# Routing by one scan with ScalarE making half of the token tables, and the weights of layers 2 and 3 set up inside neighbouring stages

## The chip, the cores and the metric

The kernel runs on one core of a Trainium2 chip. The metric is the device time of one execution in microseconds (us), lower is better. The kernel before takes 7486.76 us, the median of three runs from 7485.75 to 7492.47.

The engines are TensorE (PE, with its weight loads as PEld), VectorE (DVE), ScalarE (ACT), GpSimd (POOL) and SyncE (SP, which here only issues DMAs).

## The reference, cut to what matters

A graph network of four layers on 3125 nodes with 256 features and 50,000 edges. Each layer adds a graph convolution and a linear-attention mixer to `x`, and then a mixture of experts. Only the parts below are touched.

```python
# every layer ends in experts; layer 1 keeps 1 expert per token, the others 2
def moe(x, gate_w, gate_b, w1, b1, w2, b2):          # 8 experts, 16 in layer 2
    logits = x @ gate_w + gate_b
    vals, idx = top_k(weights_of(logits), TOP)
    # layer 1 only: pos = cumsum(one_hot) - 1; kept = pos < capacity
    return sum(vals[:, k] * expert[idx[:, k]](x) for k in range(TOP))

# layer 2 (graph part): h = x @ Wn.T + bn; the score of an edge needs sum(h[src] * attn)
# layer 3 (graph part), for l in range(2), 32 heads of 8, two edge types:
#   k = x @ Wk[l]; q = x @ Wq[l]; v = x @ Wv[l]
#   kw = k[src] times Watt[l] of the edge's type;  m = v[src] times Wmsg[l] of that type
#   a  = (kw * q[dst]).sum(-1) * pri[l, type] / sqrt(8); softmax over the edges of dst
#   h  = (softmax-weighted sum of m) @ Wa[l]
#   x  = h * sigmoid(skip[l]) + x * (1 - sigmoid(skip[l]))
```

The kernel folds the attention vector of layer 2 into a column of the node weights (`w[:, :, D+1] = sum(Wn * attn)`), and the small matrices of layer 3 into its node weights (`Wk` times the block-diagonal `Watt`, `Wv` times the block-diagonal `Wmsg`), so that one matmul over the nodes makes the whole table that the edges gather from. These folds are the "set-up" in this document.

## The kernel before

The program is a sequence of phases (`Phase`). A phase opens on-chip memory and semaphores and mostly holds one block, in which each engine has its own instruction list; at the end of a block all engines meet. Once more than 90 semaphores have been used up, the next phase begins with two more meetings, between which POOL clears them (L89 to L91). There is no planner: the order on each engine is the order in which the code issues, and engines wait for each other by semaphores only.

The 3125 nodes lie as 25 tiles of 125 partitions (`NT`, `P`). The order of stages is: layer 0 (edge sort, two graph passes), experts 0, layer 1, experts 1, layer 2, experts 2, layer 3 (two graph passes and a mixer), experts 3. The experts are `moe` (L2138), in this order:

- `settle` (a call of `renew`, L1804; names f0_in, f1_in, f2_in, f3_in, of which the profile shows f_in): per tile the mixer's matmul, the layer norm, the gate's logits. SP first loads the gate's weights, and then per tile stores the normalised rows to DRAM (L1888, L1889). DVE, ACT and PE take turns on each tile.
- `choose` (L2195) on DVE alone: maximum and index per tile, one-hot tables `oh`, their sum `ohs`, and the running count of tokens per expert over the tiles, `before`, by 25 additions with a drain after each (L2224 to L2227).
- `rank`: three matmuls and a run of small DVE instructions, which give each token its place in the list ordered by experts.
- `invert` (L2306): turns places into the list of tokens. DVE makes `hot` (which column of the list, one long comparison, L2330) and then, in five parts, `low` (which row, L2335) and `high` (L2339), that is `hot` times the tile's number and `hot` times the row's number within the tile, one instruction per half and per k. After each part PE runs its matmuls over `low` and `high` (L2322). DVE then copies the sum out and combines the halves (L2344, L2346).
- `experts`: POOL gathers the tokens (L2389), SP loads the weights, PE, ACT and DVE work through the tiles of 128 tokens.
- `fetch` (`renew` again): POOL gathers each node's results, and the next layer's table is made.

The set-up of layer 2 (`open_layer2`, L2881) stands between the end of layer 1 and f1_in, as phases of their own: two small fills (L2888), three loads by SP (`move`, L1119), a fourth load, and the fold on DVE (`attended`, L1360 to L1372). The set-up of layer 3 (`open_layer3`, L3019) stands between the end of layer 2 and f2_in: POOL makes two masks (`head_mask`, L1654), SP issues 30 loads and waits for them (L1129), POOL makes `hot` (L3049), ACT the sigmoid (L3052), PE and DVE `pcol` (L1688, L1701), and in the phase `l3_prod` DVE makes 16 products of mask and matrix (L3066) and scales 8 of them (L3072), PE runs 32 matmuls in eight groups (L3089), and DVE and ACT copy the groups out by turns (L3079, L3096).

## Time and profile before

| | |
|---|---|
| median of three runs | 7486.76 us |
| the profiled execution | 7480.89 us |
| its span | 7479.1 us |
| busy share of PE, PEld, DVE, ACT, POOL | 68, 48, 64, 38, 47% |
| mean granted TensorE clock | 0.856 of full speed |

The stretches that the change touches, as the timeline gives them, in us from the start of the span:

| stretch | from | to | length |
|---|---|---|---|
| experts 0: f0_in; choose and rank; invert | 2285.6 | 2388.7 | 103.1 |
| layer 2 set-up | 3288.0 | 3300.4 | 12.4 |
| experts 1: f1_in; choose and rank; invert | 3300.4 | 3370.0 | about 70 |
| layer 3 set-up | 4435.4 | 4479.5 | 44.1 |
| experts 2: f2_in; choose and rank; invert | 4479.5 | 4580.4 | 100.9 |
| experts 3: choose and rank; invert | 7184.4 | 7233.2 | 48.8 |

The profile is one execution, with every instruction's start and duration. Busy shares are averages over a sequence of stages with different limits, so for a change like this one it is the timeline of each stretch that matters: who works, who waits, and what the next phase waits for.

### The profile page before, as it was taken

To read this page: it belongs to the slowest core of one execution; us is meant where nothing else is said; L and a number is where in the kernel's file an instruction comes from. 1 tells how busy PE (TensorE), PEld (TensorE's weight loads), DVE (VectorE), ACT (ScalarE), POOL (GpSimd) and SP (SyncE) were. 2 spreads that over 40 slices of the span, in tenths; PEclk is the share of its full clock that TensorE was granted. 3 is DMA by queue.
4 is the path that set the end of the run, shared out by engine and by line. 5 is a ranking of instruction groups with operands and counts; after the bars stand their busy time and mean duration, and the time that the engine had idled before them with its cause. 6 is when DMAs were issued, how large, how long until landed. Compare 5 with 4: busy or idle time off the path is not lost. (4 is left out here: it accounts for less than half of the span.)

```text
span 7479.1 us, 108245 instructions
## 1 busy us (share of the span) xinstructions
PE 5106.3 (68%) x21553; PEld 3606.0 (48%) x21554; DVE 4782.9 (64%) x12016; ACT 2809.2 (38%) x6885; POOL 3492.6 (47%) x3516
## 2 busy tenths in 40 slices
PE   4763677767774967759666656967776867776764
PEld 4762444444444834548543345834444444444453
DVE  6875477677776168551556554169997459996453
ACT  2551355345524220012223212227775147772321
POOL 1775277447730267731167701136664046661014
PEclk9999877777777988979867778989998999997777
DMA  3442244334422943338334405947765157772036
GB/s 88 163 144 62 78 129 127 81 89 128 127 58 88 318 113 101 104 72 323 117 96 108 104 16 175 301 144 213 211 210 157 36 161 212 211 212 57 20 110 202
DMA packets 523816, 1021.67 MB, mean 137 GB/s; under 512 B 143645, under 2 KB 284498, under 8 KB 514846
## 3 DMA queue, kind: packets, MB, share of 16 engines
q0 software_dynamic: 191360, 489.21, 24.3%
q1 hardware_dynamic: 301663, 497.07, 20.8%
q10 hardware_dynamic: 30528, 32.52, 1.2%
q8 instruction: 87, 1.43, 0.1%
q14 instruction: 178, 1.46, 0.1%
HBM read 927.97 MB, written 90.27 MB: 136 GB/s over the span
## 5 line engine op out<-in xcount | busy, mean ns | idle before, releaser
L733 POOL DMA_INDIRECT l_hgt_ep_g<-l_tkm,l_hgt_ep_ix x832 | 922.6, 1109 | 440.7 <-PE l_hgt_ep_out L831 235.4
L744 POOL DMA_INDIRECT l_gat_ep_g<-l_gat_th,keep_e_src x832 | 861.6, 1036 | 433.8 <-issue 229.7
L831 PE MATMUL l_gat_ep_out<-l_gat_ep_g,l_gat_ep_here 128*126 128x264 f32 x1664 | 711.7, 572 | 140.1 <-DVE l_gat_acc L988 136.0
L831 PEld LDWEIGHTS l_gat_ep_out<-l_gat_ep_g,l_gat_ep_here 128*126 128x126 f32 x1664 | 393.0, 267 | 367.5 <-DVE l_gat_acc L988 299.0
L2438 DVE TENSOR_TENSOR f_moe_experts_yb<-f_moe_experts_py,f_moe_experts_b2s 128x256 f32<-128x256 f32 x208 | 88.3, 424 | 709.9 <-PE f_moe_experts_py L2421 687.6
L2389 POOL DMA_INDIRECT f_moe_experts_xg<-f_moe_tx,f_moe_tok x208 | 196.7, 945 | 734.6 <-PE f_moe_experts_px L2402 618.0
L831 PE MATMUL l_hgt_ep_out<-l_hgt_ep_g,l_hgt_ep_here 128*126 128x288 f32 x1664 | 499.5, 424 | 53.2 <-DVE l_hgt_ep_g L974 52.0
L2453 ACT ACTIVATE f_moe_experts_ht<-f_moe_experts_phid,f_moe_experts_b1b 128x128 f32<-128x128 f32 x848 | 241.3, 372 | 726.8 <-PE f_moe_experts_phid L2412 720.1
L872 ACT COPY l_gat_ep_stage<-l_gat_ep_out 30x264 f32<-30x264 f32 x832 | 307.5, 371 | 537.6 <-PE l_gat_ep_out L831 529.1
L525 POOL DMA_INDIRECT recs<-place_stage,place_pos x392 | 425.2, 1085 | 138.5 <-issue 117.7
L2710 POOL DMA_INDIRECT l_edges_g<-l_table,keep_e_src x416 | 409.7, 985 | 147.5 <-issue 120.3
L2412 PE MATMUL f_moe_experts_phid<-f_moe_experts_xt,f_moe_experts_w1b 128*128 128x128 f32 x3392 | 430.7, 281 | 66.9 <-DMA f_moe_experts_b1b<-in_L_ffn_b 63.3
L744 POOL DMA_INDIRECT l_ep_g<-l_table,keep_e_src x416 | 403.7, 970 | 126.6 <-issue 122.0
L2412 PEld LDWEIGHTS f_moe_experts_phid<-f_moe_experts_xt,f_moe_experts_w1b 128*128 128x128 f32 x3392 | 403.5, 195 | 90.6 <-issue 60.3
L805 PE MATMUL l_hgt_ep_found<-l_q,l_hgt_ep_hot 125*128 x1664 | 427.2, 401 | 23.8 <-ACT l_hgt_ep_hot L848 18.7
L831 PE MATMUL l_ep_out<-l_ep_g,l_ep_here 128*126 128x257 f32 x832 | 333.1, 553 | 106.8 <-DVE l_acc L988 99.6
L2421 PE MATMUL f_moe_experts_py<-f_moe_experts_w2b,f_moe_experts_ht 128*128 128x256 f32 x1696 | 400.0, 380 | 0.0
L872 ACT COPY l_hgt_ep_stage<-l_hgt_ep_out 126x288 f32<-126x288 f32 x832 | 307.4, 394 | 218.0 <-PE l_hgt_ep_out L831 207.3
L988 DVE TENSOR_TENSOR l_gat_acc<-l_gat_acc,l_gat_ep_out 125x264 f32 x832 | 343.9, 413 | 68.6 <-issue 48.8
L988 DVE TENSOR_TENSOR l_hgt_acc<-l_hgt_acc,l_hgt_ep_stage 125x288 f32 x832 | 369.6, 444 | 24.3 <-ACT l_hgt_ep_stage L872 17.4
L831 PEld LDWEIGHTS l_hgt_ep_out<-l_hgt_ep_g,l_hgt_ep_here 128*126 128x126 f32 x1664 | 284.6, 190 | 180.1 <-issue 132.5
L2722 PE MATMUL l_edges_out<-l_edges_g,l_edges_here 128*125 128x256 f32 x832 | 258.1, 461 | 147.9 <-DMA l_edges_g<-l_table,keep_e_src 46.3
(635 smaller groups left out, 11735.3 us busy)
## 6 DMA issues: line engine op xcount, KB each, us to landing
l_hgt_ep_hot<-locrow SPq DMA_DIRECT2D x208, 256.0 KB, 5.0
f_moe_experts_w1b<-in_L_ffn_w SPq DMA_DIRECT2D x32, 1024.0 KB
f_moe_experts_w2b<-in_L_ffn_w SPq DMA_DIRECT2D x32, 1024.0 KB
f_moe_experts_w1b<-in_L_ffn_w SPq DMA_DIRECT2D x64, 512.0 KB
f_moe_experts_w2b<-in_L_ffn_w SPq DMA_DIRECT2D x64, 512.0 KB
f_moe_experts_w1b<-in_L_ffn_W SPq DMA_DIRECT2D x56, 512.0 KB, 4.9
f_moe_experts_w2b<-in_L_ffn_W SPq DMA_DIRECT2D x56, 512.0 KB, 5.1
l_gat_ep_hot<-locrow SPq DMA_DIRECT2D x104, 256.0 KB
```

Source lines behind the costliest of these rows:

```text
L525: gp.indirect_dma_start(recs, bass.IndirectOffsetOnAxis(ap=pos[:, b, j:j + 1].bitcast(U32), axis=0), stage[:, b, j, :], None).then_inc(sca ...
L733: gp.indirect_dma_start(g[:, b % NB, j, 0:W], None, table, bass.IndirectOffsetOnAxis(ap=ix[:, b, j:j + 1].bitcast(U32), axis=0)).then_inc( ...
L744: gp.indirect_dma_start(g[:, k % NB, j, 0:W], None, table, bass.IndirectOffsetOnAxis(ap=idx[:, k * CT + j:k * CT + j + 1].bitcast(U32), ax ...
L805: mm = pe.matmul(found[:, h, j * D:j * D + D], hot[0:P, b % 2, 128 * (h * HT + j):128 * (h * HT + j) + 128], look[:, bass.ds(blks[h * HT + ...
L831: pe.matmul(out[:, t % 4, 0:WO], here[:, b % 2, t, :], g[:, b, t, F:F + WO], start=True, stop=True).then_inc(s_out, 1)
L872: act.copy(stage[lo:P + 1, b % 2, t, :], out[lo:P + 1, t % 4, 0:WO]).then_inc(s_staged, 1)
L988: v.tensor_tensor(slot, slot, stage[0:P, b % 2, t, :] if kind == "hgt" else out[0:P, t % 4, 0:WO], ALU.add).then_inc(s_added, 1)
L2412: mm = pe.matmul(phid[:, b % 2, 128 * f:128 * f + 128], w1b[:, b, k, 128 * f:128 * f + 128], xt[:, b % 2, k, :], start=(k == 0), stop=(k = ...
L2421: mm = pe.matmul(py[:, b % 2, 0:D], ht[:, b % 2, f, :], w2b[:, b, f, :], start=(f == 0), stop=(f == FC - 1))
L2453: act.activation(ht[:, b % 2, f, :], phid[:, b % 2, 128 * f:128 * f + 128], func, bias=b1b[:, b, f:f + 1])
L2710: gp.indirect_dma_start(g[:, i % RB, j, :], None, table, bass.IndirectOffsetOnAxis(ap=core.e_src[:, i * EG + j:i * EG + j + 1].bitcast(U32 ...
L2722: pe.matmul(out[:, j, 0:D], here[:, i % 4, j, :], g[:, i % RB, j, :], start=True, stop=True).then_inc(s_out, 1)
```

## The change

1. Running counts: `before` is laid out expert by expert with one leading zero each, and made by one `tensor_tensor_scan` (state times `going` plus `coming`; `going` is 0 at each expert's first column and 1 elsewhere). The two matmuls that read `before` now read it with a stride.
2. Token tables: ACT makes the half of `high` that holds the row number, one instruction per part, as soon as `hot` stands (`s_high`); DVE keeps the other half. PE waits for both.
3. Layer 2: the four loads are issued by SP at the head of f1_in, behind the gate's; the fills and the fold stand at the end of f1_in's DVE list.
4. Layer 3: the 30 loads are issued by SP at the head of f2_in, behind the gate's; everything else stands inside the invert phase of experts 2. POOL makes masks and the 16 products, ACT the sigmoid, `pcol`, all scalings and all eight copies, PE the matmul for `pcol` ahead of its token matmuls and the 32 others behind them.

```diff
 def renew(..., square=None, beside=None):
@@ SP's list, after the gate's loads
+                if beside is not None:
+                    beside["load"](sp)
...
@@ end of DVE's list
+            if beside is not None and "last" in beside:
+                beside["last"](v)
+                v.drain()
...
@@ choose
+                v.memset(coming[:, :, 0:1], 0.0)
+                v.memset(going[:, :, :], 1.0)
+                come = coming[:, :, 1:NT + 1].rearrange("p e t -> p t e")
                 if TOP == 2:
                     v.tensor_tensor(ohs[:, :, :], oh[:, 0, :, :], oh[:, 1, :, :], ALU.add)
+                    v.tensor_tensor(come, oh[:, 0, :, :], oh[:, 1, :, :], ALU.add)
                 else:
                     v.tensor_copy(ohs[:, :, :], oh[:, 0, :, :])
-                v.memset(before[:, 0, :], 0.0)
-                v.drain()
-                for t in range(NT):
-                    v.tensor_tensor(before[:, t + 1, :], before[:, t, :], ohs[:, t, :], ALU.add)
-                    v.drain()
+                    v.tensor_copy(come, oh[:, 0, :, :])
+                v.drain()
+                v.memset(going[:, :, 0:1], 0.0)
+                v.drain()
+                v.tensor_tensor_scan(before[...], going[...], coming[...], 0.0, ALU.mult, ALU.add)
+                v.drain()
...
@@ rank
-                    pe.matmul(pa[:, 0:NT * NE], core.ones[0:P, 0:P], before[:, 0:NT, :].rearrange("p t e -> p (t e)"), ...)
-                    pe.matmul(pb[:, 0:NE], core.ones[0:P, 0:P], before[:, NT, :], start=True, stop=True).then_inc(s_mm, 1)
+                    pe.matmul(pa[...], core.ones[0:P, 0:P], before[:, :, 0:NT].rearrange("p e t -> p t e"), ...)
+                    pe.matmul(pb[:, 0:NE], core.ones[0:P, 0:P], before[:, :, NT], start=True, stop=True).then_inc(s_mm, 1)
...
@@ invert
+                @block.scalar
+                def _(act):
+                    if making is not None:
+                        making["act_first"](act, p_col)
+                    act.wait_ge(s_high, 1)
+                    for q in range(NQ):
+                        act.activation(high[:, q, :, 1, :], hot[:, q * TQ * TOP:(q + 1) * TQ * TOP, :], ACT.Copy, scale=core.iotap[0:P, 0:1]).then_inc(s_rowed, 1)
+                    if making is not None:
+                        making["act_last"](act, p_prod)
                 @block.tensor
                 def _(pe):
+                    if making is not None:
+                        making["tensor_first"](pe, p_col)
                     for q in range(NQ):
                         pe.wait_ge(s_hot, q + 1)
+                        pe.wait_ge(s_rowed, q + 1)
...
+                    if making is not None:
+                        making["tensor"](pe, p_prod)
                 @block.vector
-                    v.tensor_scalar(ids[:, :, 1], core.ones[0:P, 0:NT], core.iotap[0:P, :], None, ALU.mult)
...
-                        for w in range(2):
-                            for k in range(TOP):
-                                v.tensor_tensor(high[:, q, k::TOP, w, :], hot[...], ids[..., w:w + 1]..., ALU.mult)
+                        for k in range(TOP):
+                            v.tensor_tensor(high[:, q, k::TOP, 0, :], hot[...], ids[...]..., ALU.mult)
...
@@ open_layer2: the phases l2_one, l2_w_in and l2_att give way to load (4 DMAs) and
+    def fold(v):
+        count_column(v)
+        v.wait_ge(s_in, 64)
+        v.tensor_tensor(tmp[:, :, :], w[:, :, 0:D], arow[:, :].unsqueeze(1).to_broadcast([128, 2, D]), ALU.mult)
+        v.drain()
+        v.tensor_reduce(w[:, :, D + 1:D + 2], tmp[:, :, :], AX.X, ALU.add)
+        v.drain()
+        v.tensor_tensor(tmp[0:P, 0, :], b[:, 0:D], arow[0:P, :], ALU.mult)
+        v.drain()
+        v.tensor_reduce(b[:, D + 1:D + 2], tmp[0:P, 0, :], AX.X, ALU.add)
...
@@ open_layer3: the phases l3_m8a, l3_m8b, l3_in, l3_hot, l3_alpha, l3_pcol and l3_prod give way to
+    def load(sp):
+        for to, src in pairs:                      # the same 30 transfers
+            sp.dma_start(to, src).then_inc(s_in, 16)
+    def on_pool(gp):
+        gp.affine_select(out=hot..., in_=core.ones[0:16, :]..., ...).then_inc(s_hot, 1)
+        # two memsets and four affine_selects for the masks, then
+        gp.wait_ge(s_mask, 2)
+        gp.wait_ge(s_in, 16 * len(pairs))
+        for l in range(2):
+            for i in range(2):
+                for t in range(2):
+                    for c in range(2):
+                        gp.tensor_tensor(bd[:, l, i, t, c, :]..., m8[:, i, :]..., tt[:, l, i, t, c, :]..., ALU.mult).then_inc(s_bd, 1)
+    def on_tensor_first(pe, p_col):
+        pe.wait_ge(s_hot, 1)
+        pe.wait_ge(s_in, 16 * len(pairs))
+        pe.matmul(p_col[:, 0:8], hot[:, :], pri[...], start=True, stop=True).then_inc(s_pcol, 1)
+    def on_tensor(pe, p_prod):
+        for n in range(8):
+            l, r, t = n // 4, n // 2 % 2, n % 2
+            if n % 4 == 0:
+                pe.wait_ge(s_scaled, 4 * (l + 1))
+                pe.wait_ge(s_bd, 8 * (l + 1))
+            if n >= 4:
+                pe.wait_ge(s_out, n - 3)
+            ...                                    # the same 4 matmuls as before, into p_prod[:, n % 4]
+            mm.then_inc(s_mm, 1)
+    def on_act_first(act, p_col):
+        act.wait_ge(s_in, 16 * len(pairs))
+        act.activation(alpha[:, :, 0], alpha[:, :, 0], ACT.Sigmoid)
+        act.wait_ge(s_pcol, 1)
+        act.copy(pcol[:, :], p_col[:, 0:8])
+        act.drain()
+        act.activation(alpha[:, :, 1], alpha[:, :, 0], ACT.Identity, bias=core.ones[:, 0:1], scale=-1.0)
+    def on_act_last(act, p_prod):
+        for l in range(2):
+            act.activation(wa[l][:, :, :], wa[l][:, :, :], ACT.Copy, scale=alpha[:, l, 0:1])
+            act.wait_ge(s_bd, 8 * l + 4)
+            # four products of l scaled by their column of pcol, each .then_inc(s_scaled, 1)
+        for n in range(8):
+            act.wait_ge(s_mm, n + 1)
+            act.copy(w[n // 4][...], p_prod[:, n % 4, :]).then_inc(s_out, 1)
+        act.drain()
```

## Rows read from the trace of the kernel before

**Rows 1.** Windows: busy us of PE, PEld, DVE, ACT, POOL; clock, DMA share, GB/s.

```profile
4435.40:4479.50 44.10, 10.01 (x66) 9.75 (x66) 8.88 (x33) 3.83 (x6) 2.41 (x7) 0.57 0.18 50
...
4479.50:4528.00 48.50, 45.97 (x300) 38.90 (x300) 33.72 (x151) 37.85 (x101) 0.00 (x0) 1.00 0.24 68
...
2285.00:2341.00 56.00, 50.67 (x300) 40.28 (x300) 41.79 (x176) 38.34 (x101) 0.31 (x1) 0.96 0.21 59
...
4558.00:4581.00 23.00, 6.24 (x50) 4.92 (x50) 19.72 (x30) 0.00 (x0) 0.00 (x0) 0.50 0.00 1
```

**Rows 2.** The timeline of layer 3's set-up: start, duration, engine, line, operation.

```profile
4428.60 6.83 DVE L3005 SCALAR_TENSOR_TENSOR keep_x<-l_acc,keep_x 125x6400 f32<-125x6400 f32 x1
...
4436.03 0.40 POOL L1667 TENSOR_SCALAR_AFFINE_SELECT l_m8a_b<-l_m8a_a 128x128 f32<-128x128 f32 x1
...
4438.62 0.83 SPq L1129 DMA_DIRECT2D l_alpha<-in_L_gnn_skip  x2
...
4451.97 0.98 SPq L1129 DMA_DIRECT2D l_wa<-in_L_gnn_Wa  x2
...
4469.14 9.44 PE L3089 MATMUL l_prod_acc<-l_mats_bd,l_mats_wt 128*128 128x128 f32 x64 [7.34 <-DVEq L3073]
...
4478.62 0.59 ACT L3096 COPY l_w<-l_prod_acc 128x512 f32<-128x512 f32 x1 [1.20 <-PE l_prod_acc L3089]
...
4479.51 0.37 SPq L1871 DMA_DIRECT2D f_moe_gate_gw<-in_L_ffn_gate_w  x1
```

**Rows 3.** The timeline of layer 2's set-up.

```profile
3281.14 6.83 DVE L2871 SCALAR_TENSOR_TENSOR keep_x<-l_acc,keep_x 125x6400 f32<-125x6400 f32 x1
...
3297.55 0.69 DVE L1363 TENSOR_TENSOR l_tmp<-l_w,l_arow 128x512 f32<-128x512 f32 x1 [9.09 <-PEq L95]
...
3300.36 0.37 SPq L1871 DMA_DIRECT2D f_moe_gate_gw<-in_L_ffn_gate_w  x1
```

**Rows 4.** The timeline of the running counts, experts 0 and 2.

```profile
2353.03 5.97 DVE L2226 TENSOR_TENSOR f_moe_route_before<-f_moe_route_before,f_moe_route_ohs 125x8 f32<-125x8 f32 x25
...
4536.47 6.17 DVE L2226 TENSOR_TENSOR f_moe_route_before<-f_moe_route_before,f_moe_route_ohs 125x16 f32<-125x16 f32 x25
```

**Rows 5.** The groups of DVE, by shape: the scans of two lengths.

```profile
L1070 DVE TENSOR_TENSOR_SCAN l_gat_ej_fwd<-l_gat_ej_rule,l_gat_ej_vals 4x832 f32<-4x832 f32 x2 | 3.8, 1878 | 0.2
...
L936 DVE TENSOR_TENSOR_SCAN l_gat_ep_top<-l_gat_ep_masks,l_gat_ep_fwd 32x128 f32<-32x128 f32 x104 | 43.0, 413 | 9.7 <-issue 0.4
```

**Rows 6.** The timeline of the invert phases of experts 0, 1 and 2.

```profile
2372.82 1.52 DVE L2339 TENSOR_TENSOR f_moe_invert_high<-f_moe_invert_hot,f_moe_invert_ids 125x280 bf16<-125x280 bf16 x4
...
3362.46 0.55 DVE L2339 TENSOR_TENSOR f_moe_invert_high<-f_moe_invert_hot,f_moe_invert_ids 125x160 bf16<-125x160 bf16 x2
...
4558.42 0.23 DVE L2329 TENSOR_SCALAR f_moe_invert_ids<-keep_ones,keep_iotap 125x25 f32<-125x25 f32 x1
...
4563.53 1.69 DVE L2339 TENSOR_TENSOR f_moe_invert_high<-f_moe_invert_hot,f_moe_invert_ids 125x320 bf16<-125x320 bf16 x4
...
4578.17 1.25 PE L2322 MATMUL f_moe_invert_tok<-f_moe_invert_high,f_moe_invert_low 125*128 125x128 bf16 x10 [1.97 <-DVEq L2341]
...
4580.39 0.35 ACTq L2445 DMA_DIRECT2D f_moe_experts_b2s<-in_L_ffn_b  x1
```

**Rows 7.** The groups of ACT, by shape.

```profile
L846 ACT ACTIVATE l_gat_ep_hot<-l_gat_ep_hot,keep_minusp 128x1024 bf16<-128x1024 bf16 x104 | 119.3, 1148 | 51.6 <-DMA l_gat_ep_hot<-locrow 49.2
```

**Rows 8.** The timeline of layer 3's first graph pass, POOL beside DVE.

```profile
5104.42 1.22 DVE L974 TENSOR_TENSOR l_hgt_ep_g<-l_hgt_ep_g 128x1024 f32<-128x1024 f32 x1
...
5104.71 1.74 POOL L733 DMA_INDIRECT l_hgt_ep_g<-l_tkm,l_hgt_ep_ix  x1 [0.30 <-issue]
...
5106.76 0.95 POOL L733 DMA_INDIRECT l_hgt_ep_g<-l_tkm,l_hgt_ep_ix  x1 [0.30 <-issue]
```

**Rows 9.** The timeline: PE's first mixer matmuls in f0_in and in f2_in.

```profile
2286.85 2.07 PE L1933 MATMUL f_in_out<-keep_mix_a,f_in_xt 128*125 128x256 f32 x4
...
4480.48 1.13 PE L1933 MATMUL f_in_out<-keep_mix_a,f_in_xt 128*125 128x256 f32 x4 [0.30 <-ACT f_in_xt L1974]
```

More of the change, by code:

```diff
@@ L3043, in open_layer3 @@
              + [(wa[l][:, :, :], ins["L3_gnn_Wa"][l].rearrange("(k p) m -> p k m", p=128)) for l in range(2)])
-        with Phase(core, "l3_hot") as p2:
-            block = p2.block()
-            @block.gpsimd
-            def _(gp):
-                gp.affine_select(out=hot[:, :].rearrange("h (b w) -> h b w", w=8), in_=core.ones[0:16, :].rearrange("h (b w) -> h b w", w=8),
-                                 compare_op=ALU.is_equal, fill=0.0, base=0, pattern=[[-1, 16], [0, 8]], channel_multiplier=1)
-                gp.drain()
@@ new lines, in on_tensor_first @@
+    def on_tensor_first(pe, p_col):
+        pe.wait_ge(s_hot, 1)
+        pe.wait_ge(s_in, 16 * len(pairs))
+        pe.matmul(p_col[:, 0:8], hot[:, :], pri[:, :, :].rearrange("h l c -> h (l c)"), start=True, stop=True).then_inc(s_pcol, 1)
+    def on_tensor(pe, p_prod):
[6 more added lines that the diff above has]
+                pe.wait_ge(s_out, n - 3)
+            for i in range(2):
+                for c in range(2):
+                    mm = pe.matmul(p_prod[:, n % 4, D * i + 128 * c:D * i + 128 * c + 128], wt[:, l, i, c, 128 * r:128 * r + 128], bd[:, l, i, t, c, :],
+                                   start=True, stop=True)
+            mm.then_inc(s_mm, 1)
@@ new lines, in on_act_first @@
+    def on_act_first(act, p_col):
[9 more added lines that the diff above has]
+            act.wait_ge(s_bd, 8 * l + 4)
+            for t in range(2):
+                for c in range(2):
+                    at = 4 * l + 2 * c + t
+                    act.activation(bd[:, l, 0, t, c, :], bd[:, l, 0, t, c, :], ACT.Copy, scale=pcol[:, at:at + 1]).then_inc(s_scaled, 1)
+        for n in range(8):
+            act.wait_ge(s_mm, n + 1)
+            act.copy(w[n // 4][:, n // 2 % 2, 512 * (n % 2):512 * (n % 2) + 512], p_prod[:, n % 4, :]).then_inc(s_out, 1)
+        act.drain()
@@ L3186, in build @@
             o = open_layer2(core, p2) if last > 4 else None
-            layer1_ffn(core, settle("f1_in", {}), fetch("f1_out", 4, o))
+            layer1_ffn(core, settle("f1_in", {"beside": o["fold"]} if o else {}), fetch("f1_out", 4, o))
             if last == 4:
@@ L3193, in build @@
         with Phase(core, "l3") as p3:
-            o = open_layer3(core, p3) if last > 6 else None
-            layer2_ffn(core, settle("f2_in", source), fetch("f2_out", 6, o))
+            with Phase(core, "l3_brief") as p3b:
+                o = open_layer3(core, p3, p3b) if last > 6 else None
+                making = o["making"] if o else None
+                layer2_ffn(core, settle("f2_in", {**source, "beside": making} if making else source), fetch("f2_out", 6, o), making)
             if last == 6:
```

142 lines of the change are left out of this document (65 added, 77 removed).

## The prediction

> **What bounds the kernel now.** Everything the change touches stands in serial stretches, where one engine works and the others wait at the end of the phase, so shares over the span say nothing. I read the windows first, then the timeline of each stretch, and then looked up prices for new instructions in the groups by shape. In the windows the reader is to see three kinds of stretch [rows 1]. The layer 3 set-up, 44.1 us, has no engine busy above 10.0 us: it is a chain of hand-overs and a wait for DMAs. Invert 2, 23.0 us, is DVE alone: 19.7 us of DVE, 6.2 of PE, nothing on ACT and POOL, at the half level of the clock (0.50, 1.2 GHz). f2_in, 48.5 us, is PE-heavy (46.0 us) at the full level. The edge passes, most of the span, are not touched.
>
> **Layer 3 set-up: what goes.** It runs from the end of the last DVE pass, 4428.60 + 6.83 = 4435.43, to f2_in's first instruction at 4479.51 [rows 2]: 44.1 us. One meeting of the engines stays (4478.62 + 0.59 to 4479.51, 0.3 us). Gone: 43.8 us. Three costs come back.
>
> SP in f2_in: 30 issues now stand ahead of the stores of the normalised rows. They took 4438.62 to 4452.95, 0.48 us each [rows 2], 14.3 us. Nobody in f2_in waits for a store, only the gathers behind invert 2 do. With 50 stores at the same price SP needs 80 x 0.48 = 38 us in a stage of 48.5 us, and ends in time. Cost 0; if the issues were slower by more than a quarter, SP would end last and each further tenth would cost 4 us.
>
> The cover of PE's clock: f2_in today follows the set-up's 9.4 us of matmuls and starts at the full level, afterwards PE comes from at least 7 us of idleness beside DVE's last pass (it has no work there). f0_in starts like that: its first four mixer matmuls take 2.07 us against 1.13 in f2_in [rows 9], and its stage has 0.96 of the clock on average [rows 1]. Cost 1.0 us, with 0 and 3 as ends.
>
> The matmuls of the products: they now start when the last token matmul of invert 2 is done, and end the phase. Today the run from their first start to the next phase, 4469.14 to 4479.51, takes 10.4 us, the change of the clock level within it included [rows 2]. It takes the place of the tail from 4578.17 + 1.25 to 4580.39, 1.0 us [rows 6], in which DVE's two last instructions stood; these fall in its shadow. Cost 9.4 us; 8.5 if the token matmuls before have already brought the clock up, 18 if it stays at the half level.
>
> **Layer 2 set-up.** From 3281.14 + 6.83 = 3287.97 to 3300.36, 12.4 us, less one meeting of 0.3 [rows 3]: 12.1 us go. The fold, 3297.55 to 3300.36 less the meeting, 2.5 us, and two fills of 0.1 in all come back at the end of f1_in's DVE list, where DVE is last anyway: fully on the path. Its loads were issued 30 us before, and four more issues at 0.48 on SP's queue fit ahead of the first store. Gain 9.5 us, 8.5 to 9.9.
>
> **Running counts.** 25 additions with their drains: 5.97 us with 8 experts, 6.17 with 16 [rows 4]; a fill of 0.1 goes with them. New are a second sum, written expert by expert, two more fills, a drain, and the scan. The trace has scans: 832 columns in 1.88 us, 128 in 0.413 [rows 5], so 2.08 ns a column, and 0.58 us for 8 x 26 = 208, 1.01 us for 416. The sum: 0.24 us for the smallest instruction with its drain (5.97/25) and 1.07 ns a column (6.83/6400) [rows 2] give 0.45 for 200 and 0.67 for 400. The rest is 0.4 with the scan's drain. With 8 experts 6.07 - 1.43 = 4.6 us, with 16 6.27 - 2.08 = 4.2 us: 3 x 4.6 + 4.2 = 18.0 us. All of it is on the path: PE waits in the next phase. Two unknowns: the sum's strided write and the strided read of `before` by PE. No row has either; if each took twice its time, 0.5 us per expert stage would be lost, so 16 to 18.5.
>
> **Token tables.** DVE's `high` takes 1.52 us per part in experts 0 (and 3, the same shape), 0.55 in experts 1, 1.69 in experts 2 [rows 6]. Half goes, five times, and the second column of `ids` with it (0.1): 3.9 + 3.9 + 1.5 + 4.3 = 13.6 us. ACT must keep up: 1024 columns in bf16 take it 1.148 us [rows 7], so 640 at most that, and by columns 0.72 us; DVE still needs 1.4 for `low` and 0.8 for its half, 2.2 per part, and ACT starts as soon as `hot` stands. ACT finishes each part first even at 1.15 us. Ends: 0 gain if ACT took over 3 us, 14.
>
> **Invert 2, four engines at once.** ACT's first piece (sigmoid with its table load, the `pcol` copy) needs about 2.5 us, and `hot` alone holds ACT back for 3.6 us, so it hides. POOL: two fills and five masks at 0.40 [rows 2], 2.4 us, then 16 products. The trace has no product on POOL. From below a mask of the same size, 0.40 us; from above 1.74 us, a POOL instruction that a DVE instruction stretched [rows 8]. I take 0.5, nearest to the mask, so POOL would end at 10.4 us of the phase. PE needs the first half of the products (and ACT's four scalings, at most 0.4 each) when the token matmuls end: 4578.17 + 1.25 - 4558.4 = 21.0 us today, less 4.3, so at 16.7, and the second half five us later. Products of up to 1.2 us would hide.
>
> But they do not run alone. A POOL instruction started 0.3 us after a DVE product of two on-chip tensors takes 1.74 us where its like takes 0.95, also beside other DVE work: it ends 0.95 - 0.14 us after that DVE instruction did [rows 8]. DVE's `hot`, `low` and `high` are of that kind, 16 instructions, and POOL reads on-chip too in 20 of its own. The row shows POOL held, not DVE. If only POOL is held and gets in between DVE's instructions, it ends late, at about 19 to 22 us, and PE waits 0 to 2 us. If DVE is held as well, once per instruction, 16 x 0.45 = 7 us go onto its path. I take 4 us, the ends are 0 and 8.
>
> The Trainium skill has a rule for this, and it speaks against the change: SBUF — State Buffer, section "Who interferes with whom", says that a VectorE instruction with two SBUF inputs contends with a GpSimd instruction that reads SBUF, and that whichever starts first has the shared pair to itself until it ends. The trace agrees for one direction, with 1.74 against 0.95 us; by the rule DVE is held too, which is the end of 7 us above. GPSIMD Engine Reference, section 3.1, gives a two-input product on GpSimd as 1.96 times VectorE's time; no run here shows it so far, and by it the products would still be under 1.2 us, with the sum unchanged.
>
> Clearing of semaphores: the change uses some ten more semaphores and has fewer phases, so a clearing moves and perhaps one is added; none to two of about 2 us, both signs; I take 0.
>
> **The sum.** Layer 3: 43.8 - 9.4 - 1.0 - 4.0 = 29.4. Layer 2: 9.5. Counts: 18.0. Tables: 13.6. Together 70.5 us. The profiled execution took 7480.9 us (its span is 7479.1), so it would take 7410.4. It lay 5.9 us below the median of 7486.8; against that median the forecast is 7416.3, and I say 7416. Under 0.2% (15 us) a measurement of this kernel can hardly tell from no change; the forecast is five times that.
>
> **The rivals.**
> A, the sum, with POOL and DVE holding each other up by 0 to 8 us: 7410 to 7423. Chance 0.68.
> B, ACT becomes the bound of the token tables, or the split buys nothing, because ACT reads and writes these strided rows at over 2 us a part. Against it stand 1.148 us for 1024 columns [rows 7]. 13.6 us less: 7430. Chance 0.06.
> C, PE stays at the half level in f2_in. For it: the idleness before. Against it: f0_in, with the same work per tile after a longer wait, had 0.96 on average [rows 1]. At the half level its 46 us of PE work take up to 2.07/1.13 times as long [rows 9], 84 us instead of 46, 38 us more: 7454. Chance 0.04.
> D, the level of the long graph passes moves by itself, in either direction, for a reason that this trace can't tell beforehand: I allow 15 us either way. It speaks against this that none of their instructions is touched. Chance 0.19.
> E, slower: POOL's chain ends invert 2. Its end is 2.4 + 16 T + 5.6 us after the phase's start (T a product, 5.6 half of the 9.44 us of matmuls with the last copy and the meeting), against 31 us in my sum (22.0 - 1.0 - 4.3 + 10.4 + 4). It costs from T = 1.4 on and has eaten the whole gain at T = (31 + 70.5 - 8)/16 = 5.8 us, over three times the longest price above, even with each product behind a `low` of 1.4 us. With T = 7 the kernel would take 7505. Chance 0.03.
>
> The range: A from 7408 and D's half on either side, B inside, C and E left out: 7399 to 7438. Faster by over 0.2%: A, B, C, most of D, 0.95. Within 0.2%: 0.03. Slower: 0.02 to 0.03, with E.
>
> **What would show it.** The groups: the 100 additions of the running counts gone and four scans in their place, of 0.6 and 1.0 us. The timeline: f1_in starts 0.3 to 0.4 us after layer 1's last DVE pass and f2_in after layer 2's; f1_in has a tail of 2.6 us on DVE. In invert 0 and 3 DVE's parts come every 2.3 us instead of 3.05, and PE waits for DVE, not for ACT. In invert 2 the start of the products' matmuls, 16.7 us after the phase's start if nobody holds DVE, up to 24 if it is held; POOL's products 0.4 to 0.6 us when alone, and 1 to 2 us where they start inside a `low`. The windows: clock near 1.00 in f2_in. I would be wrong if ACT or POOL, not DVE, released PE's first matmul in an invert phase, if f2_in grew by more than 3 us, or if an edge pass changed by more than 5.

## The result, and the profile after

The changed kernel takes 7430.15 us (median of 4 runs, 7422.14 to 7436.22), the kernel before, timed with it, 7487.92 us (4 runs, 7485.75 to 7492.47): a ratio of 0.9918, 95% interval 0.9906 to 0.9931. So 57.8 us are gained where 70.5 were forecast; 7430 lies inside the forecast's range of 7399 to 7438, 14 us above its 7416 and outside the 7410 to 7423 of its main case, rival A. By the interval the gain is 52 to 70 us. The profiled execution of the changed kernel took 7426.5 us, its span 7424.3, the mean granted clock 0.857 against 0.856.

The windows of the changed stages (start and end; length; busy us and count of PE, PEld, DVE, ACT, POOL; granted clock, DMA share, GB/s): invert 0, f1_in with its fold, f2_in, invert 2, invert 3.

```profile
2367.60:2386.20 18.60, 5.58 (x50) 4.39 (x50) 14.70 (x19) 3.37 (x5) 0.00 (x0) 0.50 0.00 0
3282.50:3323.50 41.00, 29.37 (x150) 28.86 (x150) 26.76 (x137) 29.34 (x78) 0.00 (x0) 0.50 0.34 99
4416.80:4467.30 50.50, 48.12 (x300) 40.87 (x300) 33.78 (x152) 38.01 (x101) 0.00 (x0) 0.94 0.38 108
4494.20:4523.00 28.80, 15.11 (x116) 13.76 (x116) 18.23 (x19) 13.94 (x27) 20.08 (x23) 0.62 0.00 1
7154.60:7171.50 16.90, 5.58 (x50) 4.39 (x50) 14.71 (x19) 3.37 (x5) 0.00 (x0) 0.50 0.00 1
```

Invert 2 now has all four engines at work; it took 22.1 us, from 4558.3 to 4580.4 (its window in [rows 1] is drawn a little wider), and takes 28.8. f2_in went from 48.8 to 50.5 us and from a clock of 1.00 to 0.94 [rows 1].

The timeline where the two set-ups stood (start, duration, engine, line, operation; in brackets the idle time before it and what ended it): the end of layer 1 and f1_in, then the end of layer 2 and f2_in.

```profile
3275.37 6.83 DVE L2905 SCALAR_TENSOR_TENSOR keep_x<-l_acc,keep_x 125x6400 f32<-125x6400 f32 x1
3282.53 0.39 SPq L1871 DMA_DIRECT2D f_moe_gate_gw<-in_L_ffn_gate_w  x1
...
3315.97 0.69 DVE L2937 TENSOR_TENSOR l_tmp<-l_w,l_arow 128x512 f32<-128x512 f32 x1
...
3317.99 0.42 DVE L2943 TENSOR_REDUCE l_b<-l_tmp 125x1 f32<-125x256 f32 x1
...
4409.67 6.83 DVE L3055 SCALAR_TENSOR_TENSOR keep_x<-l_acc,keep_x 125x6400 f32<-125x6400 f32 x1
4416.81 0.40 SPq L1871 DMA_DIRECT2D f_moe_gate_gw<-in_L_ffn_gate_w  x1
...
4418.03 2.07 PE L1935 MATMUL f_in_out<-keep_mix_a,f_in_xt 128*125 128x256 f32 x4
```

From the end of the DVE pass to the next stage there are now 0.3 us in both places, against 44.1 [rows 2] and 12.4 [rows 3]. The last line also shows the cold start of f2_in: 2.07 us for its first four matmuls, as f0_in had it [rows 9].

The running counts, experts 0 (208 columns) and experts 2 (416), where [rows 4] had 5.97 and 6.17 us: the second sum and the scan.

```profile
2357.35 0.54 DVE L2231 TENSOR_TENSOR f_moe_route_coming<-f_moe_route_oh 125x200 f32<-125x200 f32 x1
...
2358.14 0.59 DVE L2238 TENSOR_TENSOR_SCAN f_moe_route_before<-f_moe_route_going,f_moe_route_coming 125x208 f32<-125x208 f32 x1
...
4475.68 0.89 DVE L2231 TENSOR_TENSOR f_moe_route_coming<-f_moe_route_oh 125x400 f32<-125x400 f32 x1
...
4476.83 1.02 DVE L2238 TENSOR_TENSOR_SCAN f_moe_route_before<-f_moe_route_going,f_moe_route_coming 125x416 f32<-125x416 f32 x1
```

The timeline of invert 2. The reader is to see three things: the two masks of POOL (L3107) that end only after DVE's `hot` (the first 0.26 us after it, the second as long after the first `low`), the pairs of `high` at 1.41 us, and the products' matmuls (L3137) that start behind the last token matmul and end the phase.

```profile
4494.42 3.48 DVE L2365 TENSOR_TENSOR f_moe_invert_hot<-keep_iota,f_moe_route_hi 125x3200 bf16<-125x3200 f32 x1
...
4494.82 4.92 POOL L3107 TENSOR_SCALAR_AFFINE_SELECT l_brief_wide<-l_brief_wide 128x128 f32<-128x128 f32 x2
...
4497.93 3.70 ACT L2344 ACTIVATE f_moe_invert_high<-f_moe_invert_hot,keep_iotap 125x640 bf16<-125x640 bf16 x5 [1.88 <-DVE f_moe_invert_hot L2365]
...
4500.88 13.49 POOL L3119 TENSOR_TENSOR l_brief_bd<-l_brief_m,l_brief_tt 128x128 f32<-128x128 f32 x16
...
4502.06 1.41 DVE L2373 TENSOR_TENSOR f_moe_invert_high<-f_moe_invert_hot,f_moe_invert_ids 125x320 bf16<-125x320 bf16 x2
...
4512.49 1.25 PE L2356 MATMUL f_moe_invert_tok<-f_moe_invert_high,f_moe_invert_low 125*128 125x128 bf16 x10 [1.73 <-DVEq L2375]
4512.75 1.28 ACT L3156 ACTIVATE l_brief_bd<-l_brief_bd,l_brief_pcol 128x128 f32<-128x128 f32 x4 [5.39 <-POOL l_brief_bd L3119]
4513.53 8.48 PE L3137 MATMUL f_moe_invert_p_prod<-l_brief_bd,l_brief_wt 128*128 128x128 f32 x64
...
4522.06 0.58 ACT L3159 COPY l_w<-f_moe_invert_p_prod 128x512 f32<-128x512 f32 x1 [0.31 <-PE f_moe_invert_p_prod L3137]
4522.97 0.35 ACTq L2479 DMA_DIRECT2D f_moe_experts_b2s<-in_L_ffn_b  x1
```

In all invert phases it is DVE (the queue entry behind `high`, L2375) that releases PE; in invert 2 ACT's five instructions take 3.70 us together, 0.74 each, and are done with the last part while DVE makes its second.

**Stage by stage.** I cut both timelines at the first instruction of each stage. The stretches that the change touches, in us (before minus after): running counts with the rank phases behind them 4.8, 4.0, 3.2, 4.8 = 16.8; inverts 0, 1 and 3, 2.1, -0.3 and 3.7; set-ups 12.1 and 42.8; the ends paid for them -2.1 (f1_in), -1.7 (f2_in) and -6.7 (invert 2). That is 66.7. The clearing of semaphores (L90), six times in both kernels, has moved from the experts to the ends of inverts 0 and 1 (1.6 us each, so these lose 3.7 and 1.3 in truth), and from the layer 3 set-up to the end of layer 2's pass, 1.7 us. With these put right the change removes 68 us by the stretches it touches, where the span fell by 54.8. The untouched stretches grew by 13 in sum. Layer 3's two graph passes, called hgt0 and hgt1 below, moved against each other, in the kernel before and in the changed one:

```profile
5033.70:5777.00 743.30, 513.83 (x1872) 320.49 (x1872) 663.38 (x1145) 515.03 (x1249) 486.63 (x518) 0.97 0.68 203
6060.50:6790.40 729.90, 508.55 (x1872) 316.82 (x1873) 663.30 (x1145) 513.21 (x1248) 486.43 (x518) 0.99 0.70 206
...
4974.40:5711.50 737.10, 513.90 (x1872) 320.52 (x1872) 662.90 (x1145) 514.60 (x1249) 493.58 (x518) 0.97 0.69 204
5996.60:6735.40 738.80, 513.06 (x1872) 320.79 (x1872) 663.85 (x1145) 514.18 (x1248) 485.88 (x518) 0.98 0.69 204
```

hgt0 is 6.2 us shorter, 1.7 of it a clearing that has moved out of it into the stage before; hgt1 is 8.9 longer. Of the others experts 3 grew most, by 6.3 us, at 267 GB/s against 277, and experts 2 shrank by 3.7. Where this comes from is what the experiments ask, besides the contention in invert 2.

### The profile page after: what moved, and what is told of

Its sections match the earlier page's. It is cut to its first block and busy times, and to the rows that moved or that the text cites. A ratio compares the mean times of both kernels' runs of the same rounds, so it can differ in the third digit from the quotient of the medians.

```text
span 7424.3 us, 107945 instructions
## 1 busy us (share of the span) xinstructions
PE 5125.7 (69%) x21553; PEld 3617.6 (49%) x21554; DVE 4752.9 (64%) x11861; ACT 2828.9 (38%) x6921; POOL 3525.0 (47%) x3532
## 5 line engine op out<-in xcount | busy, mean ns | idle before, releaser
L805 PE MATMUL l_hgt_ep_found<-l_q,l_hgt_ep_hot 125*128 x1664 | 431.2, 404 | 25.5 <-ACT l_hgt_ep_hot L848 20.6
L805 PEld LDWEIGHTS l_hgt_ep_found<-l_q,l_hgt_ep_hot 125*128 125x128 f32 x1664 | 310.5, 197 | 99.2 <-issue 62.0
```

The source lines that it names most:

```text
L805: mm = pe.matmul(found[:, h, j * D:j * D + D], hot[0:P, b % 2, 128 * (h * HT + j):128 * (h * HT + j) + 128], look[:, bass.ds(blks[h * HT + ...
```

## The experiments

Each is timed against the kernel before on the same chip in the same series; "stretch" is the time between the first instructions of two stages in the one profiled execution.

**Four parts alone**, each on the kernel before: the choose and rank edits; the invert edits without the layer 3 work; the loads and fold of layer 2; those of layer 3, with DVE still making both halves of `high`:

```diff
+                        for w in range(2):
+                            for k in range(TOP):
+                                v.tensor_tensor(high[:, q, k::TOP, w, :], hot[:, q * TQ * TOP + k:(q + 1) * TQ * TOP:TOP, :],
+                                                ids[:, q * TQ:(q + 1) * TQ, w:w + 1].to_broadcast([P, TQ, TT]), ALU.mult)
```

> The kernel before with the running counts alone changed (scan in the four choose phases). Theory S (the gain is the sum of the touched stretches): the stretches choose to rank of the two profiles say 4.6 + 4.2 + 3.3 + 4.9 = 17.0 us, the forecast said 18.0; so 16 to 18 us under the kernel before, 7470 +- 3, and the passes hgt1 and experts 3 as in the kernel before, within 3 us. Rival D (the drift of the untouched passes comes with the change): hgt1 +8.9 and experts 3 +6.3 us again, and the time only 2 to 8 us under the kernel before.

> The kernel before with the token tables alone split between VectorE and ScalarE. The forecast's term is 13.6 us; the stretches of the two profiles had 2.1 (invert 0), -0.3 (invert 1) and 3.7 us (invert 3), with a clearing of semaphores of about 1.6 us that had moved into inverts 0 and 1. Theory S: the clearing is elsewhere here, so 3.7 + 1.3 + 4.0 + 3.7 = 12.7 us, time 10 to 14 us under the kernel before. Rival B (the split buys little where ScalarE is slow): under 6 us. Rival D: drift of hgt1 and experts 3 by +15 us, time the same as before.

> The kernel before with the layer 2 set-up alone moved into f1_in. Theory S: -12.1 us in front of f1_in, +2.1 to 2.6 at its end, so 9.5 to 10 us under the kernel before. Rival (f1_in's stores come late behind the four loads, or drift): 5 us or less.

> The kernel before with the layer 3 set-up alone moved (loads in f2_in, products in invert 2, VectorE still making both halves of the token tables). Theory S: -42.8 us in front of f2_in, +1.7 in f2_in; invert 2 grows by 28.8 - 22.1 + 4.0 = 10.7 us if the table split and the making add up, so 28 to 31 us under the kernel before. VectorE is held by GpSimd only while it makes one half more per part: if each two-input instruction is held once, 2 us more. Rival D (the drift belongs to the moved weights of layer 3: hgt1 +8.9, experts 3 +6.3): 15 us under the kernel before.

| part alone | stretches, clearings put right, us | by the measured time, us | ratio, 95% interval |
|---|---|---|---|
| counts | -17.7 | -14.2 | 0.9982 (0.9973 to 0.9991) |
| token tables | -12.3 | +4.2 | 1.0007 (0.9997 to 1.0017) |
| layer 2 | -10.0 | +4.6 | 1.0005 (0.9996 to 1.0014) |
| layer 3 | -26.3 | -20.6 | 0.9977 (0.9966 to 0.9988) |

Three of the four came as theory S had them (17.0, 12.7 and 9.5 to 10 us), layer 3 did not, with 26.3 us for 28 to 31: choose -4.7, -4.5, -3.4, -4.9; inverts of the tables -2.1 (a clearing of 1.6 in it), -1.0, -3.8, -3.7; the gap before f1_in gone and +2.1 behind it; the gap before f2_in -42.6, f2_in +1.4, invert 2 +12.9. They add up to -66.3, close to the 68 of the whole. The time does not: the parts give -26.0 together, against -57.8 for the whole, and the tables and layer 2 give nothing that can be measured. By the intervals the gain is 7 to 20 us for the counts, which holds their 17.7 (the median, 7469.9, is the 7470 expected), at most 2 for the tables, 3 for layer 2 and 25 for layer 3; these three lie under their stretches. Rival B is out, since ACT's split saved what was expected in its stretches. What eats the gain stands in passes without an edited instruction. The windows of layer 2's graph pass, in the kernel before and with the tables alone:

```profile
3762.30:4352.70 590.40, 377.70 (x1044) 230.31 (x1044) 355.02 (x1154) 166.71 (x471) 403.68 (x416) 0.69 0.38 96
```

```profile
3753.80:4355.90 602.10, 384.55 (x1044) 234.92 (x1044) 355.29 (x1154) 166.71 (x471) 404.05 (x416) 0.67 0.37 94
```

The same 1044 matmuls, 1154 DVE and 416 POOL instructions take 11.7 us longer (1.7 of it a clearing that now stands at the end), at a clock of 0.67 against 0.69 and with the same DVE and POOL time. The expectation for p_counts that hgt1 and experts 3 stay within 3 us failed: +6.5 and +6.5.

In p_l3 invert 2 grew by 12.9 us, not 10.7 (the 2 us more that its expectation allowed if each instruction is held), and its DVE rows give the price of the contention. First a part with POOL's products running, then the last one, when they had ended (4533.66 + 13.41 = 4547.07):

```profile
4543.24 1.54 DVE L2359 TENSOR_TENSOR f_moe_invert_low<-keep_iota,f_moe_route_lo 125x1280 bf16<-125x1280 f32 x1
4544.70 2.72 DVE L2363 TENSOR_TENSOR f_moe_invert_high<-f_moe_invert_hot,f_moe_invert_ids 125x320 bf16<-125x320 bf16 x4
4547.54 1.49 DVE L2359 TENSOR_TENSOR f_moe_invert_low<-keep_iota,f_moe_route_lo 125x1280 bf16<-125x1280 f32 x1
4548.95 1.69 DVE L2363 TENSOR_TENSOR f_moe_invert_high<-f_moe_invert_hot,f_moe_invert_ids 125x320 bf16<-125x320 bf16 x4
```

So four `high` cost 1.03 us more beside POOL, 0.26 each, and a `low` 0.05.

**The changed kernel again, and its work moved further.** after_again has no edit. pool_early starts POOL's list in f2_in; choose also takes the rest out of invert 2; choose110 is choose with fewer clearings:

```diff
+        if beside is not None and "pool" in beside:      # in renew (f2_in)
+            @block.gpsimd
+            def _(gp):
+                beside["pool"](gp)
...
-                        making["pool"](gp)                # in invert
```

```diff
+            with Phase(core, f"{name}_choose") as pc:     # choose, beside DVE's list
...
+                        making["act_first"](act, p_col)
+                        making["act_last"](act, p_prod)
...
+                        making["tensor_first"](pe, p_col)
+                        making["tensor"](pe, p_prod)
...
-        if len(self.core.spent) > 90:                     # choose110
+        if len(self.core.spent) > 110:
```

> The changed kernel once more, nothing edited. The four parts alone gave 14.2, -4.2, -4.6 and 20.6 us, 26.0 together, against 57.8 for the whole and about 65 for the touched stretches of the two profiles. Theory N (the edge and expert passes scatter from execution to execution by 10 us and more, a stretch that the change touches does not): the touched stretches repeat within 0.5 us, the untouched ones of the same kernel differ by up to 10 us each way, and the time is 50 to 65 us under the kernel before. Rival F (each kernel has its own fixed offset in the untouched passes): hgt1 +8.9 and experts 3 +6.3 us repeat within 2 us.

> The changed kernel with GpSimd's masks and its 16 products moved out of invert 2 into f2_in, where it has nothing to do. Theory H (VectorE is held in invert 2 by GpSimd's products, about 0.5 us in four to five parts): invert 2 goes from 28.8 to 26.0 to 26.6 us, the last token matmul comes 2.3 us earlier, and f2_in, bound by TensorE, grows by less than 1 us; time 1 to 3 us under the changed kernel. Rival (the longer periods come from ScalarE or TensorE, not from GpSimd): the periods of VectorE's parts stay at 2.95 us and invert 2 at 28.8. Second rival: GpSimd holds VectorE in f2_in as well, and that stage grows by over 2 us.

> As the last, and ScalarE's scalings, the 32 product matmuls and the copies of their results moved out of invert 2 into the choose phase in front of it, where TensorE and ScalarE are idle for 14.5 us. Theory: invert 2 is then the token tables alone, 22.1 - 4.3 = 17.8 to 18.5 us instead of 28.8; the choose phase must hold sigmoid and pcol (2 us), eight scalings and 9.5 us of matmuls at the half level, about 14 to 16 us against 14.5, so 0 to 2 us more. Net 9 to 11 us under the changed kernel, 7420 by its own median. Rival: the matmuls run at the half level for the whole and end at 18 us, so choose grows by 4 us and 6 to 7 are left.

> As the last, with the spent semaphores cleared when over 110, not 90, have gathered, so fewer clearings. Theory: each clearing is two meetings and a clearing, about 1.6 us, all on the path; one or two of six go and none need stand in an invert phase, 1.5 to 3.5 us less than the last. Rival: the clearings lie in places where something else is waited for (a DMA) and the time does not change.

| | median us | runs from, to | ratio to before (7483.02), 95% interval |
|---|---|---|---|
| after_again | 7429.39 | 7426.64, 7433.21 | 0.9929 (0.9916 to 0.9943) |
| pool_early | 7421.65 | 7410.30, 7429.95 | 0.9920 (0.9907 to 0.9934) |
| choose | 7415.02 | 7409.15, 7420.36 | 0.9907 (0.9892 to 0.9922) |
| choose110 | 7418.92 | 7402.91, 7431.69 | 0.9915 (0.9901 to 0.9929) |

after_again: the touched stretches repeat within 0.1 us; of the untouched ones hgt1 repeats (738.8 both times), experts 2 is 4.0 longer, experts 3 2.3 shorter, layer 2's pass 2.6 longer. Both theories had a part right. Two profiles of one kernel differ by a few us per pass, but hgt1's excess over the first profile of before (8.9) returned in after_again, choose (9.1), p_tables (9.8), p_l2 (7.8), pool_early (7.5) and p_counts (6.5), and was 2.9 in p_l3 and 0.8 in choose110. In the same runs hgt0, the clearing put right, came 3.4 to 5.4 us shorter, and 0.5 in choose110. The two passes together are 1.4 to 6.3 us longer than in the first profile of before, 0.2 in choose110, and in p_l3 2 shorter: most of hgt1's excess stands against hgt0, and hgt1 alone does not explain the missing gain.

pool_early, the timeline: POOL's products in f2_in, then the last part of invert 2 and PE's matmuls.

```profile
4438.31 6.68 POOL L3120 TENSOR_TENSOR l_brief_bd<-l_brief_m,l_brief_tt 128x128 f32<-128x128 f32 x16 [19.56 <-DMA l_wa<-in_L_gnn_Wa]
...
4509.23 0.89 DVE L2374 TENSOR_TENSOR f_moe_invert_high<-f_moe_invert_hot,f_moe_invert_ids 125x320 bf16<-125x320 bf16 x2
...
4510.20 1.25 PE L2357 MATMUL f_moe_invert_tok<-f_moe_invert_high,f_moe_invert_low 125*128 125x128 bf16 x10 [1.17 <-DVEq L2376]
4511.24 9.50 PE L3138 MATMUL f_moe_invert_p_prod<-l_brief_bd,l_brief_wt 128*128 128x128 f32 x64
```

With POOL away a pair of `high` is back at 0.89 us from 1.41, the period of a part at 2.41 from 2.98, and the last token matmuls come 15.7 us after the phase's start, not 18.35: theory H, with 2.6 us. The phase shrinks only by 1.6, for the products' matmuls now take 9.50 us against 8.48. The windows show why, first two of the changed kernel, then two of pool_early:

```profile
4513.50:4515.80 2.30, 2.30 (x14) 2.30 (x12) 0.59 (x2) 0.74 (x3) 0.86 (x3) 0.50 0.00 0
4515.90:4522.60 6.70, 6.12 (x55) 5.93 (x53) 0.00 (x0) 4.33 (x8) 0.00 (x0) 1.00 0.00 0
...
4511.20:4515.70 4.50, 4.50 (x24) 4.50 (x22) 0.52 (x2) 1.17 (x2) 0.00 (x0) 0.50 0.00 0
4515.80:4521.30 5.50, 4.93 (x45) 4.74 (x43) 0.00 (x0) 3.46 (x6) 0.00 (x0) 1.00 0.00 0
```

The granted clock rises to the full level at nearly the same time in both, 21.7 and 21.2 us after the phase's start, so the matmuls that now come earlier run at the half level. By the measured time pool_early is 7.7 us under after_again, with overlapping runs; the 1.1 us of its stretches are below what that can tell. f2_in grew by 0.5 us. POOL's products alone take 0.42 us each from start to start, 0.84 in invert 2.

choose: the windows of f2_in, the choose phase and invert 2.

```profile
4413.90:4465.50 51.60, 48.84 (x300) 41.08 (x300) 34.31 (x152) 38.22 (x102) 8.77 (x23) 0.93 0.37 106
4465.50:4483.40 17.90, 10.22 (x67) 10.00 (x67) 10.72 (x89) 11.53 (x24) 0.00 (x0) 0.77 0.00 1
4495.00:4512.90 17.90, 6.24 (x50) 4.92 (x50) 15.53 (x19) 3.70 (x5) 0.00 (x0) 0.50 0.00 0
```

Invert 2 is at 17.9 us as expected, but the choose phase grew by 3.4 us, which is nearer to the rival's 4: ACT did the sigmoid, its table load and the scaling of `wa` first, and PE started only 3.7 us into the phase. By the measured time choose is 14.4 us under the changed kernel of the same series, and their runs do not overlap; its stretches account for 8 of them. choose110 saved its 1.6 us in invert 0 and in invert 1 and one clearing in all, but by the measured time it is no faster than choose (the runs overlap): 1.7 us are below what that can tell.

**Controls on the kernel before, and the best version.** before_again has no edit; b_110 only the new threshold; b_double makes the additions twice; best is choose with ACT's order changed and the threshold at 125:

```diff
-                for t in range(NT):                      # b_double
+                for t in [*range(NT), *range(NT)]:
                     v.tensor_tensor(before[:, t + 1, :], before[:, t, :], ohs[:, t, :], ALU.add)
```

```diff
-        act.activation(alpha[:, :, 0], alpha[:, :, 0], ACT.Sigmoid)
         act.wait_ge(s_pcol, 1)
         act.copy(pcol[:, :], p_col[:, 0:8])
...
                     act.activation(bd[:, l, 0, t, c, :], bd[:, l, 0, t, c, :], ACT.Copy, scale=pcol[:, at:at + 1]).then_inc(s_scaled, 1)
+        act.activation(alpha[:, :, 0], alpha[:, :, 0], ACT.Sigmoid)
```

> The kernel before once more, nothing edited, profiled a second time. In eight profiles of kernels that share their untouched passes with it, hgt0 came 4 to 7 us shorter and hgt1 7 to 10 us longer than in the first profile of the kernel before, except in one (choose110: -0.7 and +0.8). Theory N (the passes fall into one of some patterns of the granted clock in each execution, by chance): this profile may show hgt0 at 737 and hgt1 at 738 us, their sum within 3 us of 1473. Rival F (the pattern belongs to the kernel): hgt0 at 743 and hgt1 at 730 us again, within 2 us.

> The kernel before with the spent semaphores cleared at over 110 instead of 90: five clearings for six, at other places, no other instruction changed. Theory P (the untouched passes of any edited kernel stand some 9 us above those of the kernel before, on average over the seven edited ones, since their level depends on where and when the program stands, not on what is computed): one clearing less is -1.7 us, so the time is 5 to 10 us above the kernel before. Rival: the clearings alone count, and it is 2 us under it, within the measurement's 5.

> The kernel before with the 25 additions of the running counts made twice in each of the four choose phases (the result is the same). By the trace they take 5.97, 5.97, 6.17 and 5.97 us: if they are fully on the path, the four choose phases grow by 24.1 us together, each by its own 6.0, and the time by 24 us; with theory P's offset by 33. Rival (something else hides part of them): the choose phases grow by less than 20 us together.

> The kernel of the run choose with ScalarE's pcol and eight scalings ahead of the sigmoid, its table load and the scaling of wa, so that the products' matmuls start 2.2 us earlier in the choose phase, and the semaphores cleared at over 125. Theory: choose of layer 2 goes from 17.9 to 15.5 to 16 us, the clearings from six to four or five, 1.7 us each: 4 to 5.5 us under the run choose in the touched stretches, 7405 to 7415 on the clock, and faster than the changed kernel by 15 us or more. Rival: the copies of the products, behind the sigmoid on ScalarE, end the phase instead, and only the clearings are gained.

In this series the unchanged kernel took 8097.14 us (median of 29 runs, 8076.97 to 8144.64), 8% more than on the same chip 42 minutes before, so only what was run in it can be compared: before_again 8093.97 (ratio 1.0, 0.9986 to 1.0015), b_110 8100.36 (1.0004, 0.9988 to 1.0021), b_double 8122.67 (1.0031, 1.0015 to 1.0047), best 8015.38 (0.9896, 0.9875 to 0.9917). The second profile of the kernel before shows where the 8% are. Its window of layer 2's graph pass, 590.40 us above, and what was waited for in it (engine, line; us in total, times, longest):

```profile
4130.40:4901.90 771.50, 405.18 (x1044) 244.30 (x1045) 356.74 (x1154) 166.33 (x471) 402.77 (x416) 0.62 0.29 73
```

```profile
POOL l_ep_g L744 <- PE l_ep_out L831: 171.4, 33, 23.9
```

The same 416 gathers, with the same POOL time (402.77 us against 403.68), now arrive at 73 GB/s instead of 96, and POOL waits 171.4 us for PE to free a buffer, where it waited 4.6. That PE is late because rows are late is my reading; the profile gives no releaser for its new idle time. The six graph passes grew by 91, 95, 80, 181, 14 and 43 us, and the edge sort in front of them by 98. The edge sort is not a gather: ACT waited 269.4 us there for loads of 512 KB, against 198.6, and the stage moved the same 88.1 MB at 101 GB/s instead of 114. The choose, rank and invert phases of the same profile are all within 0.1 us of the first. So the graph passes and the edge sort have a level that something outside the kernel sets (no run shows what), and the choose, rank and invert phases have none. It also means that before_again could not answer its question on hgt1, nor b_110 its own (+3.2 us, interval -10 to +17: both expectations fit).

b_double: the choose phases grew by 6.4, 6.4, 6.6 and 5.7 us, 25.1 together, and the time by 25.5 (interval 12 to 38). The additions were fully on the path. best: its windows of f2_in, choose and invert 2,

```profile
4969.80:5020.90 51.10, 48.61 (x300) 40.85 (x300) 33.95 (x151) 37.99 (x101) 8.77 (x23) 0.93 0.38 107
5020.90:5036.10 15.20, 9.34 (x66) 9.09 (x66) 10.78 (x89) 11.40 (x24) 0.00 (x0) 0.83 0.01 2
5048.20:5066.20 18.00, 6.24 (x50) 4.92 (x50) 15.57 (x19) 3.70 (x5) 0.00 (x0) 0.50 0.00 0
```

show a choose phase of 15.2 us, only 0.7 over the 14.5 that it takes with nothing beside it, and there were four clearings. It is 81.8 us under the kernel before of its series. Its stretches explain that: 68 of the change, 8 of the run choose, 2.7 of ACT's order, 3.4 of two clearings, 82 together. Its ratio, 0.9896, lies under the change's 0.9918 and 0.9929, but their intervals overlap and they were not timed together; that it beats the changed kernel rests on choose, timed beside it, and on the stretches.

## Why the prediction was right, step by step

The time fell inside the range, and the mechanisms of the stretches were those forecast. The point is in part luck: 7430 lies above rival A's 7410 to 7423, and it is the very number of rival B, whose mechanism is refuted. Without rival D's allowance the range would have ended at B.

- **Layer 3's set-up.** The gap went to 0.3 us, all 43.8 of it; the stretch lost 42.8. SP's 30 loads hid, at 0.51 us an issue (4417.66 to 4433.02). The cold start of PE cost 1.7 us where 1.0 was taken (bounds 0 and 3): the first four matmuls took 2.07 as in f0_in, and the clock was 0.94 over the stage, not near the 1.00 that I wanted to see. Rival C, the half level for the whole stage, did not come.
- **Products behind the token matmuls.** 9.4 us were taken: 10.4 from the matmuls' start to the next phase, less the tail of 1.0. From the end of the last token matmul, 4513.74, to the next phase at 4522.97 it is 9.2, so the cost was 8.2, at the lower end of 8.5. The matmuls took 8.48 us for 9.44, because the full level came 2.4 us into them, against 4.3 in the kernel before. What sets this is not shown: behind the same token matmuls it came 4.5 us in (pool_early).
- **Contention in invert 2.** Taken 4, ends 0 and 8; it is 2.6 us on the path (pool_early). DVE is held as well as POOL, as the end of 7 us assumed, but not at 0.45 us an instruction: 0.26 for each `high`, 0.05 for a `low`. The invert phase grew by 6.7 where my terms gave 9.1; the line above accounts for about 1.2 of that and this one for 1.4. The Trainium skill, SBUF — State Buffer, section "Who interferes with whom", says that whichever of the two engines starts first keeps the shared pair until its instruction ends; the trace agrees in both directions: POOL's two masks (0.75 us in pool_early's f2_in) needed 4.92 us beside `hot` and the first `low`, and a pair of `high` rose from 0.89 to 1.41.
- **POOL's products.** Taken 0.5 us, found 0.42 in f2_in and 0.84 beside `low` and `high`. The last was ready at 4514.37 and ACT's last scaling at 4514.03, while PE came to the second half of its groups when the fourth was made, just before ACT's fourth copy at 4518.48. Rival E was far off. The trace before had a nearer row than the two that bounded this price, DVE's own 16 products:

```profile
4464.00 3.31 DVE L3066 TENSOR_TENSOR l_mats_bd<-l_mats_m,l_mats_tt 128x128 f32<-128x128 f32 x16
```

POOL needs 6.68 us for the same 16, 2.02 times as long, which is near the ratio for which the forecast had no run.
- **Layer 2.** 12.1 gone, 2.1 back where 2.6 was said: 10.0 for 9.5.
- **Counts.** 16.8 with the rank phases for 18.0. The scans are at the forecast's prices (0.59 and 1.02 us for 0.58 and 1.01). The strided sum takes 0.54 and 0.89 us for 0.45 and 0.67, the strided read by PE 0.05 us, and the fills more than the forecast had for them: that of `going` alone is 0.23 us for 208 columns and 0.40 for 416. This is the lower part of the 16 to 18.5 given.
- **Token tables.** 3.7, 1.3, 3.7 for 3.9, 1.5, 3.9, once the clearings are put right, and 3.8 alone (p_tables) for the 4.3 of invert 2. ACT needs 0.74 us a part in invert 2, DVE 2.98 there and 2.33 in inverts 0 and 3.
- **Clearings.** Taken 0; six before and six after. The one in layer 3's set-up was part of the 43.8 and came back as 1.7 us elsewhere, which the term of 0 missed.
- **The sum.** 68 for 70.5, in which misses of both signs cancel. The 10 to 14 us that are missing by the measured time are rival D, which I had given 15 us either way at a chance of 0.19: the term of the sum that was mis-sized is the zero for everything untouched, which measured 13 us in the profile of the result. The result alone can't tell this from noise, since its interval of 52 to 70 us holds 68; in after_again, p_tables, p_l2, p_l3 and choose110 the interval leaves the stretches out. A sign that I had named for being wrong, an edge pass changed by more than 5 us, did come, with hgt1's 8.9.
- **Where the missing gain is.** In every comparison of the result and the two series after it the time gave less than the stretches, by 3.5 (counts), 16.5 (tables), 14.6 (layer 2), 5.7 (layer 3), 10 and 14.5 (the whole), 8, 8 and 14 (pool_early, choose, choose110); in the last series by 0 (b_double and best) and 5 (b_110), each within 13 to 17 us either way. The comparisons are not independent, for those of a series share one timing of the kernel before. The traces show the place in part: graph passes at a slightly lower clock (layer 2's with the tables, 0.67 for 0.69) and experts 3 at fewer GB/s. They do not show what sets it, nor whether the lower clock is the cause: in the last series it fell to 0.62 together with the traffic. That it belongs to the kernel before, whose passes would fall well by chance, that a moved start does it, or that it is the surroundings of those two series, stays open; the last series was disturbed too much to tell.

## What to carry to other kernels

Time a serial stretch by its timeline, where an edit of 4 us repeats within 0.1 us, and let the measured time judge only the whole; a part that gains 10 us in its stretches can measure as nothing in a kernel whose untouched passes differ by as much between its variants. Work taken out of a gap is cheapest where its engine has nothing to do: the products cost 10.9 us in invert 2, beside DVE and behind PE's own matmuls, and 0.7 us in the choose phase with at most 1.1 in f2_in. When work is moved, see what the engine in front does before it gets to what others wait for: a table load, a sigmoid and the scaling of `wa` ahead of the scalings that PE needed cost 2.7 us.

## What the runs showed of the hardware

- A bf16 product of 320 columns on DVE costs 0.26 us more while POOL runs 128x128 float products, a comparison of 1280 float columns 0.05 (p_l3). POOL pays far more: two masks 4.92 us for 0.75, 16 products 13.49 for 6.68.
- A 128x128 float product on POOL takes 0.42 us from start to start (6.68 us for 16, pool_early), on DVE 0.21 (3.31 us, before). One instruction lasts 452 ns on POOL; ACT's scaling of the same size lasts 385.
- DVE writing 200 float columns expert by expert takes 0.54 us, writing them in order 0.30; 400 columns 0.89 and 0.51.
- The same kernel on the same chip took 7484 us in one series and 8097 in another; 602 of the 607 us by which their profiles differ stand in the six graph passes and the edge sort. In one pass it was 73 against 96 GB/s, with the same gathers and DVE, ACT and POOL as busy as before; PE's busy time rose with the lower clock (0.62 for 0.69), from 377.7 to 405.2 us.
